# Layer-0 scores of destination rows by TensorE, and their steps ranked ahead of dense blocks, in a four-layer GNN kernel

## The reference

```python
# layer 0: scored by a leaky relu, softmax over the edges of one destination
f   = concat(x[src], edge_attr) @ W1.T
e   = leaky_relu(concat(f, x[dst]), 0.01)
s   = e @ attn                      # attn[:64] meets f, attn[64:] meets x[dst]
h   = segment_sum((x @ W2.T)[src] * softmax_by_dst(s)) + bias
# layer 1: s = x[src] @ att_w[:64] + x[dst] @ att_w[64:], softmax by dst, then
#          messages, layer norm, an MLP with gelu, layer norm
# layer 2: messages weighted by degrees, segment sum by src, @ W.T + b
# layer 3: segment sum by src of edge_weight * x[dst]
x   = layernorm(x + layer(x))       # four times
```

## Time and profile before

| what | value |
|---|---|
| median of 3 runs | 2801.25 us (2794.16 to 2805.04) |
| span of the profiled execution | 2797.4 us (its own time is not listed apart from the runs) |
| PE busy | 1944.0 us, 69% |
| DVE busy | 1685.3 us, 60% |
| POOL busy | 1661.4 us, 59% |
| ACT busy | 1497.3 us, 54% |
| DMA | 214.75 MB, mean 77 GB/s |

### The profile page before, as it was taken

How to read it: one execution, slowest core, us unless ns; L and a number is a source line. 1 busy time by engine, 2 the same in 40 slices (tenths; PEclk the granted TensorE clock), 3 DMA queues, 4 the chain that set the end, 5 groups by cost and what they waited for, 6 DMA issues and landing times. The chain is left out here.

```text
span 2797.4 us, 27574 instructions
## 1 busy us (share of the span) xinstructions
PE 1944.0 (69%) x8422; PEld 1002.8 (36%) x8422; DVE 1685.3 (60%) x3220; ACT 1497.3 (54%) x2242; POOL 1661.4 (59%) x1610
## 2 busy tenths in 40 slices
PE   6998778679988688888999868658888875000000
PEld 3444334227643233364444327543333434000000
DVE  4876699993888578745655433997656687000002
ACT  4777667553677568746787762337777652000000
POOL 6777777600037565000777757775777768677774
PEclk9999899886999789979999996559989885555555
DMA  3233222101668674102454491442111233100002
GB/s 63 66 68 81 58 56 68 51 30 45 203 126 58 47 56 52 46 16 71 139 144 137 118 228 53 120 121 67 52 52 53 89 105 98 55 17 22 22 21 96
DMA packets 235785, 214.75 MB, mean 77 GB/s; under 512 B 156783, under 2 KB 169926, under 8 KB 235638
## 3 DMA queue, kind: packets, MB, share of 16 engines
q1 hardware_dynamic: 181190, 166.34, 20.7%
q0 software_dynamic: 51200, 46.31, 12.2%
q10 hardware_dynamic: 3248, 0.34, 0.1%
HBM read 140.36 MB, written 86.04 MB: 81 GB/s over the span
## 5 line engine op out<-in xcount | busy, mean ns | idle before, releaser
L2372 POOL DMA_INDIRECT stab<-wk,rank_i x200 | 208.5, 1042 | 289.1 <-DVE wk L588 231.4
L545 ACT ACTIVATE b_s<-ps,vec 128x512 f32<-128x512 f32 (+1 forms) x356 | 240.9, 684 | 159.4 <-PE ps L624 59.8
L2369 POOL DMA_INDIRECT u<-x2tab,dpos_i x200 | 220.8, 1104 | 82.7 <-issue 77.8
L2369 POOL DMA_INDIRECT u<-x3tab,src_i x200 | 206.1, 1030 | 85.3 <-issue 59.2
L2369 POOL DMA_INDIRECT u<-in_x_dram,src_i x200 | 201.4, 1007 | 76.7 <-issue 59.8
L2369 POOL DMA_INDIRECT e_b<-x0tab,dpos_i x72 | 72.7, 1009 | 290.9 <-DVEq L2174 265.5
L2372 POOL DMA_INDIRECT out_dram<-u,dst_i x176 | 198.2, 1126 | 74.7 <-issue 59.8
L2369 POOL DMA_INDIRECT u<-in_x_dram,dst_i x200 | 201.1, 1006 | 64.4 <-issue 59.5
L2372 POOL DMA_INDIRECT out_dram<-u,sfin_i x200 | 196.5, 982 | 66.3 <-issue 66.3
L776 DVE TENSOR_SCALAR b_x<-b_s 128x8 f32<-128x8 f32 x2 | 0.3, 168 | 389.3 <-DMA b_gl<-out_dram 389.3
L533 PE MATMUL ps<-b_h,blk_c 128*128 128x512 f32 (+1 forms) x296 | 174.4, 673 | 57.9 <-ACT b_gl L553 57.4
(11 more groups left out here) (428 smaller groups left out, 5026.4 us busy)
## 6 DMA issues: line engine op xcount, KB each, us to landing
b_gl<-in_x_dram SPq DMA_DIRECT2D x98, 256.0 KB, 2.7
wk<-dlist SPq DMA_DIRECT2D x50, 500.0 KB
wk<-slist SPq DMA_DIRECT2D x50, 500.0 KB
out_dram<-b_gl SPq DMA_DIRECT2D x93, 256.0 KB, 2.0
u<-stab SPq DMA_DIRECT2D x25, 510.0 KB
x2none<-b_gl SPq DMA_DIRECT2D x25, 250.0 KB
wk<-x2none SPq DMA_DIRECT2D x25, 240.0 KB
x2tab<-wk SPq DMA_DIRECT2D x25, 240.0 KB
```

What stands on the lines that cost most here:

```text
L545: return nc.scalar.activation(b_s[l][:, 0:w], pB[l][:, 0:w], ACT.Abs_reciprocal_sqrt, bias=col(EPSV))
L2369: pool.indirect_dma_start(out=o, out_offset=None, in_=tab, in_offset=at_ix(ix), **kw).then_inc(s, 16)
L2372: pool.indirect_dma_start(out=tab, out_offset=at_ix(ix), in_=a, in_offset=None, bounds_check=rows_n - 1, oob_is_err=False).then_inc(s, 16)
```

## The change

The scores of destination rows in layer 0 go the way of the source rows: four transposes on PE into e0, one ACT copy into `q_b`, one leaky step on DVE, four matmuls with a third column pair of `att` (it holds `attn[64:]`), one DVE copy of 125x8. The row `R_ATT0` and its load go, two small loads come. `l0` and `l0d` now share the counters of their semaphores (`nth`). And `l0`, `l0d` and `xd1` get rank 1.

```diff
-            unit(("l0", g), 2, "xt pe .68 +e0;xc act .6 -e0;et pe .4 +e0;ec act .3 -e0;f pe 2.05 +e1;fc act .6 -e1;fl dve .7;"
+            unit(("l0", g), 1, "xt pe .68 +e0;xc act .6 -e0;et pe .4 +e0;ec act .3 -e0;f pe 2.05 +e1;fc act .6 -e1;fl dve .7;"
-            unit(("l0d", g), 2, "a dve .7;b dve 1.41", [(("u2", g), "t", LANDED)] + ([(("l0d", g - 1), "b", 0)] if g else []))
+            unit(("l0d", g), 1, "xt pe .68 +e0;xc act .6 -e0;fl dve .7;s pe .5 +e0;out dve .2 -e0", [(("u2", g), "t", LANDED)] + ([(("l0d", g - 1), "s", 0)] if g else []))
-            unit(("xd1", g), 2, "a dve 1.4;sq act .65;var dve .7;rs act .3;mul dve .7;dot dve 1.45",
+            unit(("xd1", g), 1, "a dve 1.4;sq act .65;var dve .7;rs act .3;mul dve .7;dot dve 1.45",
+        def nth(step, kind, g):
+            return sorted(at[k, n][step] for k in ("l0", "l0d") for n in GROUPS).index(at[kind, g][step]) + 1
+        def l0d_pe(pe, t, g):
+            yield t["xt"]
+            pe.wait_ge(*gathered(1, g))
+            pe.wait_ge(S("e0_free"), use("e0", t["xt"]))
+            for q in range(Q):
+                last_t = nc.tensor.transpose(e0[:, P * q:P * q + P], xd[0:P, GC * g + 2 * q:GC * g + 2 * q + 2, :], ident[0:P, 0:P])
+            last_t.then_inc(S("l0_t"), 1)
+            yield t["s"]
+            pe.wait_ge(S("l0_leaky"), nth("fl", "l0d", g))
+            pe.wait_ge(S("e0_free"), use("e0", t["s"]))
+            for q in range(Q):
+                last_s = nc.tensor.matmul(e0[0:P, 2 * q:2 * q + 2], q_b[:, P * q:P * q + P], att[:, 2, :], start=True, stop=True)
+            last_s.then_inc(S("l0_s"), 1)
+        def l0d_act(act, t, g):
+            yield t["xc"]
+            act.wait_ge(S("l0_t"), nth("xt", "l0d", g))
+            if g:
+                act.wait_ge(S("l0_s"), nth("s", "l0d", g - 1))
+            else:
+                act.wait_ge(S("src_ps"), 1)
+            nc.scalar.activation(q_b[:, 0:EW], e0[:, 0:EW], ACT.Identity).then_inc(S("e0_free"), 1)
         def l0d_dve(dve, t, g):
-            yield t["a"]
-            dve.wait_ge(*gathered(1, g))
-            a = xd[0:P, GC * g:GC * g + GC, :]
-            dve.wait_ge(S("dve_step"), dotted[0])
-            k = stepped(nc.vector.scalar_tensor_tensor(t3(q_b[0:P, :]), a, 0.01, a, ALU.mult, ALU.max))
-            yield t["b"]
-            dve.wait_ge(S("dve_step"), k)
-            dot_row(dve, t3(q_b[0:P, :]), q_b, R_ATT0, g)
+            yield t["fl"]
+            dve.wait_ge(S("e0_free"), use("e0", t["xt"]) + 1)
+            nc.vector.scalar_tensor_tensor(q_b[:, 0:EW], q_b[:, 0:EW], 0.01, q_b[:, 0:EW], ALU.mult, ALU.max).then_inc(
+                S("l0_leaky"), 1)
+            yield t["out"]
+            dve.wait_ge(S("l0_s"), nth("s", "l0d", g))
+            nc.vector.tensor_copy(grp(r5c, g), e0[0:P, 0:GC]).then_inc(S("e0_free"), 1)
@@ def setup_loads
-                for m, a in ((0, attn[0:D]), (1, att_w[0:D])):
+                for m, a in ((0, attn[0:D]), (1, att_w[0:D]), (2, attn[D:2 * D])):
-            for r, a in ((R_ATT0, attn[D:2 * D]), (R_ATT1, att_w[D:2 * D]), (R_B0, bias0)):
+            for r, a in ((R_ATT1, att_w[D:2 * D]), (R_B0, bias0)):
```

More of the change, by code:

```diff
@@ L138, in gnn_resnorm_kernel @@
         w2c = sb("w2c", [128, D])
-        att = sb("att", [128, 2, 2])
+        att = sb("att", [128, 3, 2])
         vec = sb("vec", [128, 20])
         B0, G1, LB1, G2, LB2, MB2, MB1, L2B, FUS, EPSV, EPS2, CB0, CR, CT, C2, HB1, FUN = range(17)
-        rowc = sb("rowc", [128, 4, D])
-        R_ATT0, R_ATT1, R_B0, R_C2 = range(4)
+        rowc = sb("rowc", [128, 3, D])
+        R_ATT1, R_B0, R_C2 = range(3)
         neg2 = sb("neg2", [1, 2])
@@ L227, in gnn_resnorm_kernel @@
                  (";wt2 pe 1.2 +e1;wc2 dve 1.4 -e1" if m else ""),
-                 [(("l0", g), "out", 0) for g in GROUPS] + [(("l0d", g), "b", 0) for g in GROUPS] if m == 0 else
+                 [(("l0", g), "out", 0) for g in GROUPS] + [(("l0d", g), "out", 0) for g in GROUPS] if m == 0 else
                  [(("src", g), "h", 0) for g in GROUPS] + [(("xd1", g), "dot", 0) for g in GROUPS])
@@ L1050, in l0_pe @@
             yield t["s"]
-            pe.wait_ge(S("l0_leaky"), g + 1)
+            pe.wait_ge(S("l0_leaky"), nth("fl", "l0", g))
             pe.wait_ge(S("e0_free"), use("e0", t["s"]))
@@ L1055, in l0_pe @@
             last_s.then_inc(S("l0_s"), 1)
+        def l0d_pe(pe, t, g):
[11 more added lines that the diff above has]
+            last_s.then_inc(S("l0_s"), 1)
         def l0_act(act, t, g):
             yield t["xc"]
-            act.wait_ge(S("l0_t"), g + 1)
+            act.wait_ge(S("l0_t"), nth("xt", "l0", g))
             if g:
@@ L1068, in l0_act @@
             if g:
-                act.wait_ge(S("l0_leaky"), g)
+                act.wait_ge(S("l0_leaky"), nth("fl", "l0", g - 1))
             nc.scalar.activation(e_c[:, 0:EW], e1[:, 0:EW], ACT.Identity).then_inc(S("e1_free"), 1)
+        def l0d_act(act, t, g):
[6 more added lines that the diff above has]
+            nc.scalar.activation(q_b[:, 0:EW], e0[:, 0:EW], ACT.Identity).then_inc(S("e0_free"), 1)
         def l0_dve(dve, t, g):
@@ L1075, in l0_dve @@
             if g:
-                dve.wait_ge(S("l0_s"), g)
+                dve.wait_ge(S("l0_s"), nth("s", "l0", g - 1))
             nc.vector.scalar_tensor_tensor(e_d[:, 0:EW], e_c[:, 0:EW], 0.01, e_c[:, 0:EW], ALU.mult, ALU.max).then_inc(
@@ L1079, in l0_dve @@
             yield t["out"]
-            dve.wait_ge(S("l0_s"), g + 1)
+            dve.wait_ge(S("l0_s"), nth("s", "l0", g))
             nc.vector.tensor_copy(grp(score, g), e0[0:P, 0:GC]).then_inc(S("e0_free"), 1)
@@ L1355, in softmax_dve @@
             if m == 0:
-                dve.wait_ge(S("e0_free"), use("e0", at["l0", NG - 1]["s"]) + 1)
+                for kind in ("l0", "l0d"):
+                    dve.wait_ge(S("e0_free"), use("e0", at[kind, NG - 1]["s"]) + 1)
                 dve.wait_ge(S("prep_ps"), 2)
@@ L2230, in gnn_resnorm_kernel @@
         w1d, w2s, w1e_s, w1e_t, zpn = (b_gl[1][:, a:b] for a, b in ((0, 128), (128, 256), (256, 256 + DE), (384, 384 + D), (512, 640)))
-        LOADED = 16 * (2 * 7 + 2 + 2 * 3 + 2 + 4 + 1 + 1 + 2 + 3)
+        LOADED = 16 * (2 * 7 + 2 + 2 * 4 + 2 + 4 + 1 + 1 + 2 + 2)
         pio, gio, bio = (w_[7][:, 16 * j:16 * j + 16].bitcast(i32) for j in range(3))
@@ L2451, in _ @@
             pe_programs += lanes(pe, dense_pe, src_pe, dst_pe)
-            pe_programs += [l0_pe(pe, at["l0", g], g) for g in GROUPS]
+            pe_programs += [l0_pe(pe, at["l0", g], g) for g in GROUPS] + [l0d_pe(pe, at["l0d", g], g) for g in GROUPS]
             pe_programs += [softmax_pe(pe, at["sm", m], m) for m in range(2)]
@@ L2463, in _ @@
             act_programs = [setup_act(act)] + lanes(act, dense_act, src_act, dst_act)
-            act_programs += [l0_act(act, at["l0", g], g) for g in GROUPS]
+            act_programs += [l0_act(act, at["l0", g], g) for g in GROUPS] + [l0d_act(act, at["l0d", g], g) for g in GROUPS]
             act_programs += [softmax_act(act, at["sm", m], m) for m in range(2)]
```

## The result

The changed kernel took 2784.25 us (median, 2780.12 to 2790.41) against 2802.03: a ratio of 0.9939, interval 0.9912 to 0.9965. A second set of runs gave 0.993 (0.9906 to 0.9954). It is faster, by some 18 us; forecast were 37. The traced execution has a span of 2778.1 us, 19.3 less than the one before.

A forecast was written before the change was run, and what follows sets the result against it. DVE was taken as the bound ahead of the first softmax. Terms -24, -17 and +4 gave -37 on the span of 2797.4, so 2760; with the median 3.9 above the span, 2764 us, range 2738 to 2800.

The forecast's parts named there:

- A: Up to layer 0's softmax: less DVE work -31.7 us, index steps moved behind the add +5.5, PE +2; taken as -24.
- B: Layer 1's gathers through second softmax and outputs: earlier xd1 -34 us, dense instructions +6, late second output +11; -17.
- Rivals 2 and 3: Only the first-softmax gain arrives, 2781 us (chance 0.16); first add stays near 604, freed DVE waiting for PE, 2788 (0.15).
- C: Before the final scatters: dense blocks fall behind, 87 of 98 instead of 92, mostly swallowed by POOL's wait; +4 us.
- (4): At the final scatters: slower, because dense block 86's store becomes their start; 2832 us, chance 0.08.
- (5): Ahead of the first softmax: slower, small transposes and matmuls bring TensorE's clock to its low level; 2832 us, chance 0.04.

The follow-up runs named there:

- The experiment with held dense blocks: Changed kernel with no dense block entering a lane from layer 0's twentieth destination group until the first softmax's weights are made; 2953 us.
- R: Kernel before the change with only the ranks of l0 and l0d set from 2 to 1; 2801 us, ratio 0.9982.
- X: Kernel before the change with only the rank of xd1 set from 2 to 1; 2790 us, ratio 0.9956.
- RX: Kernel before the change with l0, l0d and xd1 at rank 1, layer 0's destination scores still on DVE; 2799 us, ratio 0.9992.
- the kernel with the spread index: Changed kernel with the index program's second sort planned at 1.5 us a step instead of 1.0, ending at 690 instead of 602; 2793 us, ratio 0.996.

## Why the prediction was wrong

The time lies inside the range of 2738 to 2800 by luck, not by my sum: at the end of layer 1's scatters A and B had left -2.8 us where I had -41, and what comes behind, where I had +4, brought -16.5. Rivals 2 and 3 (2781 and 2788) are nearer to 2784, by the number alone: A gave nothing, and the add did not stay near 604.

**The step that failed** is the price of A and B by DVE's work alone: I counted DVE's instructions and took its waits for PE and ACT as 2 us ahead of the first add and as unchanged elsewhere. The waits ate the gain, at three places.

- **A, the work ahead of the first add** (-31.7 forecast): -18.5 measured, -13.5 between the second traces of the two kernels. The counts were right. The place in the index program that stood at 365 stands at 368 now; from there to the add DVE is busy 200.05 of 218 us, where the earlier trace rows had 230.94 of 240: 31 us less work, but 9 us more idle, most of it for dense steps on ACT (7.9 us for L545, none in the earlier trace rows). My 2 us for "PE is next in line" were too little.
- **A, the softmax** (+5.5 for 13 index steps): I counted what was moved into the softmax on DVE and took everything else in it as unchanged. It grew by 16.2 us, and A became 0. The experiment with held dense blocks shows that it takes dense steps between its own to lengthen it; R shows that their order does most of it, without the low clock. Up to the end of its first part (the subtraction ahead of the exponential) 3.4 us were added, which is the most that the index steps can have cost there; the other 12.8 came behind it, where PE and ACT lie on the path.
- **B** (-17): -24.6 at the second add (356.8 us after the gathers' start instead of 381.5; forecast 347) and -20.8 at the first output. What is missing was lost ahead of the last source copy: it came 356.1 us after the gathers' start instead of 336.0, 20.1 more, where I had 10 for its 16 more DVE instructions. DVE's work there did grow by 9.4 us (271.3 instead of 261.9); the rest is waiting. The second output came 21.8 us behind the first: +11.8 against +11 forecast. Then the pace was 11.45 us instead of 11.26, another 4 over 23 outputs, which I had not priced. At the end of the scatters 2.8 us are left.
- **C** (+4): the sum was small for the wrong reason. Block 86's store came 31 us later in absolute time, not the 45 less what A and B bring, and just touched the final scatters (2.83 us). But what I treated as swallowing a loss, POOL's 14.54 us wait for L1628, was itself a dense wait: the message ahead of L1628 stood behind 92 dense blocks. With five of them out of its way the wait is gone, 11.8 us; in X one was enough. The sign of the term was wrong.
- **Rivals.** (4) is half true: block 86's store does become the start of the final scatters, and forbids any further gain upstream, as the 40 us waits show; it didn't come late enough to cost. (5) was wrong where I put it: the granted clock from 346 to 586 is 0.89, against 0.88 in the earlier trace rows, and the 100 new transposes ran at a median of 270 ns, as those in the earlier trace rows. Both kernels have a stretch at 0.50 near there: before from 585 to 595, ahead of the add, now from 603 to 618, in the softmax, where PE had waited 3.51 and 2.54 us for DVE. So the rule of the Trainium skill that I weighed ("TensorE: Matmul & The Clock Gate", Part 4: PE-mode transpose) is not felt in the window in which the transposes run. RX, which has the ranks without them, has a mean of 0.84 in its softmax against 0.74; whether they play a part in that no run here separates.
- **Not settled:** why the issues and the one wait in the last part of the final scatters became 7 us shorter, and how the softmax's 12.8 us divide between waits on PE and ACT, table loads and the clock.

## What to carry to other kernels

When work is taken off the engine that bounds a stage, ask what the new order puts *inside* the next stage's chain of round trips. Here the displaced index steps cost it some 3 us on DVE, but the order of the dense steps among its own on PE and ACT, which I had not counted, cost 11 and more. Where background work has a deadline (here the stores that the final scatters wait for), write down its slack beside the critical chain's: with 33 us of slack, a change that delays it by 31 has spent everything that later changes could win. And the wait in front of the last stage may be the cheapest to remove: moving three more blocks behind the deadline took the kernel with the spread index from 2793 to 2771 us.

## What the runs showed of the hardware

The granted clock of TensorE was 0.89 in the mean of the stretch with the many small matmuls (346 to 586; its windows of ten us lie between 0.56 and 1.00), as it was 0.88 before without them (0.50 to 1.00). It lay at its low level, 0.50, from 603 to 618, in the softmax, after places where PE had idled for DVE 3.51 us (up to 594.86) and 2.54 us (up to 602.04), with dense matmuls still in line; it rose again in the window from 616 to 626, where PE was busy 8.79 of 10 us. Pairs of 512-column matmuls of the same shape took 2.07 and 1.05 us on the two sides. The kernels with the spread index, which have the same order up to there, differ by up to 19 us at the start of layer 1's gathers (798.2 to 817.6), so a stage's time from one trace is good to about that, and only the repeated pattern (the softmax at 50.2 and 50.2 us) and the medians bear a verdict.
